# The first query products move into the feed-forward block, and statistics and splits change places, in a transformer kernel

## The reference, cut to what matters

```python
x = x + 0.5 * _L0_ffn_ref(_layernorm(x), ...)    # gated, 256 -> 768 -> 256
x = x + _L0_attn_ref(_layernorm(x), ...)         # 16 heads of 16
x = x + 0.5 * _L0_ffn_ref(_layernorm(x), ...)
x = x + 0.5 * _L1_ffn_ref(_layernorm(x), ...)    # gelu, 256 -> 1024 -> 256
x = x + _L1_attn_ref(_layernorm(x), ...)         # rotary, causal mask
x = x + 0.5 * _L1_ffn_ref(_layernorm(x), ...)
```

## Time and profile before

| what | value |
|---|---|
| median of 3 runs | 2131.1 us (2126.84 to 2133.12) |
| profiled execution, its own time | 2130.66 us |
| its span, first to last instruction | 2128.9 us |
| PE busy | 2003.7 us (94%) |
| DVE busy | 1652.5 us (78%) |
| ACT, POOL busy | 1317.6 us (62%), 510.8 us (24%) |
| mean granted TensorE clock | 0.976 of full speed |

### The profile page before, as it was taken

The page is one execution under the profiler, slowest core; times in us unless marked ns, Lnnn a source line. Parts: engine busy times, 40 slices in busy tenths (PEclk is TensorE's granted clock), DMA queues, the critical chain, the costliest instruction groups (busy, mean ns, idle before and its releaser), DMA issues. The chain is left out here.

```text
span 2128.9 us, 43472 instructions
## 1 busy us (share of the span) xinstructions
PE 2003.7 (94%) x16326; PEld 1246.8 (59%) x16326; DVE 1652.5 (78%) x2997; ACT 1317.6 (62%) x2560; POOL 510.8 (24%) x572
## 2 busy tenths in 40 slices
PE   4998989999999999998998999978999999989999
PEld 3887833333333333336887899864444444448998
DVE  7776699999999999937776545789999999927333
ACT  3443338888888888881444445544777777753544
POOL 2000141221241241142101211584321212122110
PEclk9999969999999999999999999997999999999999
DMA  4002844225335444313002000385465555310000
GB/s 149 1 0 81 313 87 74 47 52 100 77 67 91 73 85 79 49 51 111 1 0 65 1 0 1 114 277 117 91 113 103 118 108 104 87 54 27 20 20 30
DMA packets 124374, 161.63 MB, mean 76 GB/s; under 512 B 54668, under 2 KB 77900, under 8 KB 124180
## 3 DMA queue, kind: packets, MB, share of 16 engines
q1 hardware_dynamic: 101156, 112.32, 24.7%
q0 software_dynamic: 16256, 37.82, 6.7%
q10 hardware_dynamic: 6768, 8.91, 1.3%
HBM read 94.02 MB, written 63.70 MB: 74 GB/s over the span
## 5 line engine op out<-in xcount | busy, mean ns | idle before, releaser
L1630 ACT ACTIVATE att_probs<-att_s_exp 128x512 f32<-128x512 f32 (+3 forms) x1792 | 883.3, 551 | 201.1 <-PE att_s_exp L1528 160.0
L1665 DVE TENSOR_REDUCE maxes<-att_s_max 128x2 f32<-128x1024 f32 x640 | 771.6, 1223 | 32.6 <-PE att_s_max L1486 28.2
L1553 PE MATMUL att_o_ps<-att_probs,att_v_st 128*32 128x256 f32 (+2 forms) x6400 | 514.1, 393 | 10.2 <-ACT att_o_sb L1607 9.1
L1553 PEld LDWEIGHTS att_o_ps<-att_probs,att_v_st 128*32 128x32 f32 x6400 | 127.1, 108 | 253.1 <-issue 137.3
L1659 DVE CUSTOM_DVE_ANT_0 att_s_max<-att_s_max,mask_q 128x384 f32<-128x384 f32 (+3 forms) x512 | 235.6, 523 | 23.9 <-PE att_s_max L1486 21.6
L1528 PE MATMUL att_s_exp<-first_q,first_k 64*128 64x512 f32 (+3 forms) x672 | 177.8, 471 | 1.4 <-DMA first_q<-att_m_parts 0.8
L1486 PE MATMUL att_s_max<-first_k,first_q 62*128 62x512 f32 (+3 forms) x672 | 146.7, 435 | 22.9 <-DVE maxes L1665 11.6
L1528 PE MATMUL att_s_exp<-w_lo,w_hi 64*128 64x512 f32 x640 | 164.5, 497 | 1.2 <-DMA w_lo<-att_m_parts 1.2
L1749 POOL TENSOR_TENSOR att_m_parts<-m_turned,att_zeros 32x128 fp32r<-32x128 f32 x64 | 29.0, 453 | 496.7 <-ACT m_turned L1596 358.4
L1528 PEld LDWEIGHTS att_s_exp<-w_lo,w_hi 64*128 64x128 f32 x640 | 63.1, 183 | 133.9 <-ACT att_probs L1630 123.5
L1528 PEld LDWEIGHTS att_s_exp<-first_q,first_k 64*128 64x128 f32 x672 | 78.7, 189 | 100.5 <-ACT att_probs L1630 87.8
(11 more groups left out here) (322 smaller groups left out, 4368.2 us busy)
## 6 DMA issues: line engine op xcount, KB each, us to landing
attention_rows<-att_o_sb POOLq DMA_DIRECT2D x64, 256.0 KB, 4.5
output_wide<-attention_weights POOLq DMA_DIRECT2D x36, 256.0 KB, 5.6
first_q<-q_parts SPq DMA_DIRECT2D x132, 64.0 KB, 4.9
first_k<-k_parts SPq DMA_DIRECT2D x66, 128.0 KB, 4.5
q_parts<-qkv_parts SPq DMA_DIRECT2D x16, 512.0 KB
k_parts<-qkv_parts SPq DMA_DIRECT2D x16, 512.0 KB
att_v_raw<-v_rows SPq DMA_DIRECT2D x32, 256.0 KB, 5.7
output_o_t<-attention_rows POOLq DMA_DIRECT2D x16, 512.0 KB, 7.1
```

Source lines behind the costliest of these rows:

```text
L1553: mm = pe.matmul(o_ps[j * VW:(j + 1) * VW, cols], v_st[:, it.par, kt, j, :], probs[:, step % 2, j, cols], start=kt == 0 and opens, stop=st ...
L1630: act.activation(probs[:, step % 2, j, q0:512], s_exp[:, plan.bank[place], q0:512], ACT.Exp, scale=1.0 if causal else 0.25).then_inc(s["ex ...
L1665: v.tensor_reduce(maxes[:, qc, :, pairs, qt - 4 * qc, kc], banks, AX.X, ALU.max).then_inc(s["max_done"], 1)
```

## The change

Six things are changed at once. (1) `load_stage`: x chunk 1 is issued ahead of the gate weights. (2) POOL waits there for `xn_ready`, the first normalised chunk, before its splits. (3) In the following feed-forwards the norm steps are made for the tiles of six chunks (`FOLLOW`, 0 to 23), both in chunk 6: variance at slice 3, ahead of `part_lo`, reciprocal root at slice 5. (4) In `ffn0a` and `ffn1a` chunk 1 of the next stage is normalised before the last `finish`. (5) The accumulators `qk_ps` of the next stage are allocated around both blocks, the feed-forward's `up_ps` is a view of them, and PE makes the first two query tiles (`HEAD`) at the end of the feed-forward's block, after the test on `whole` is left. (6) `qkv_stage` and `rope_stage` start with the third tile; the norm of the last two chunks (`LATER`, 24 to 31) is split: variance in chunk 0 and root in chunk 2 of `qkv_stage`, variance in chunk 2 and root in chunk 3 of `rope_stage`.

```diff
-    body(CHUNKS - 3, 1, (CHUNKS - 3) // 2, False, False, "variance")
-    body(CHUNKS - 2, 0, (CHUNKS - 2) // 2, False, False, "rstd")
+    body(CHUNKS - 3, 1, (CHUNKS - 3) // 2, False, False)
+    body(CHUNKS - 2, 0, (CHUNKS - 2) // 2, False, False, True)
...
+FOLLOW = slice(0, 6 * CT)
+HEAD = KD
+LATER = slice(6 * CT, TILES)
...
+def qk_tile(pe, E, par, i):
+
+    w, half = (E.wq, E.wk)[i // KD], i % KD
+    for k in range(KD):
+        mm = three_pass(pe, E.qk_ps[:, i, :], pair(w, slice(None), k, slice(half * P, (half + 1) * P)),
+                        pair(E.xt, slice(None), par, k, slice(None)), k == 0, k == KD - 1)
+    return mm
...
             load_x(0)
+            load_x(1)
             split.load(sp, 0)
-            load_x(1)
...
             clear_operands(p, E)
+            p.wait_ge(s["xn_ready"], 1)
             for i in range(1, len(jobs)):
...
+        head = follow and xt_next is None
+        if head:
+            up_ps = E.qk_ps[:, 0:up_shape[1] * up_shape[2], :].rearrange("p (a g) n -> p a g n", a=2)
...
+            if head:
+                pe.wait_ge(used, CHUNKS * F)
+                pe.wait_ge(s["hi_ready"], CHUNKS * KD + KD)
+                pe.wait_ge(s["lo_ready"], CHUNKS * KD + KD)
+                pe.wait_ge(s["late_lo"], 2)
+                for i in range(HEAD):
+                    mm = qk_tile(pe, E, 0, i)
+                    if i % E.qk_step == E.qk_step - 1:
+                        mm.then_inc(E.qk_ready, 1)
...
-                    if f == 4 and follow and part == "variance":
-                        norm_variance(v, E, s["next_step"], NEXT)
-                    if f == 4 and follow and part == "rstd":
-                        norm_rstd(v, E, s["next_step"], NEXT, NORM_STEPS)
+                    if f == 3 and follow and next_norm:
+                        v.wait_ge(s["next_step"], 1)
+                        norm_variance(v, E, s["next_step"], FOLLOW, 1)
+                    if f == 5 and follow and next_norm:
+                        norm_rstd(v, E, s["next_step"], FOLLOW, 1 + NORM_STEPS)
...
+            if head:
+                v.wait_ge(s["turned"], CHUNKS * KD)
+                normalise(v, E, CHUNKS + 1, 1, s, rows=1)
             finish(CHUNKS - 1, (CHUNKS - 1) % 2)
...
 # qkv_stage
-                for i in range(QK):
+                for i in range(HEAD if first else 0, QK):
...
                 if opening(c):
-                    n = rest_variance(v, E, s)
-                    norm_rstd(v, E, s["ln_step"], REST, n)
+                    rest_variance(v, E, s, LATER)
+                elif isinstance(c, int) and c == 2:
+                    norm_rstd(v, E, s["ln_step"], LATER, 1 + NORM_STEPS)
...
 # rope_stage
-                for kind, w in enumerate((E.wq, E.wk)):
+                for kind in range(0 if c else HEAD // KD, KINDS):
...
-            count_front(v, E, s)
-            normalise(v, E, 1, 1, s)
-            n = rest_variance(v, E, s)
-            norm_rstd(v, E, s["ln_step"], REST, n)
-            v.tensor_scalar(neg_mean[:, :], E.mean[:, :], -1.0, None, ALU.mult).then_inc(s["means"], 1)
+            count_front(v, E, s, 2)
+            v.tensor_scalar(neg_mean[:, FOLLOW], E.mean[:, FOLLOW], -1.0, None, ALU.mult).then_inc(s["means"], 1)
...
+                if c == 2:
+                    n = rest_variance(v, E, s, LATER)
                 multiply(c, 1)
+                if c == 3:
+                    norm_rstd(v, E, s["ln_step"], LATER, n)
+                    v.tensor_scalar(neg_mean[:, LATER], E.mean[:, LATER], -1.0, None, ALU.mult).then_inc(s["means"], 1)
```

More of the change, by code:

```diff
@@ L492, in path @@
                     down(CHUNKS - 1, f, False)
-            if not gated:
-                path(False)
[L496 to L501, removed]
+            if gated:
+                whole = pe.value_load(E.whole[0:1, 0:1])
+                with pe.If(whole > 0):
+                    path(True)
+                with pe.Else():
+                    path(False)
+            else:
+                path(False)
+            if head:
[7 more added lines that the diff above has]
+                        mm.then_inc(E.qk_ready, 1)
         @block.scalar
@@ L594, in measure, with body @@
                     v.wait_ge(s["x_new"], c * 2 + 2)
-                    statistics(v, E, c)
-            def body(c, par, use, first, last, part=None):
+                    return statistics(v, E, c)
+            def body(c, par, use, first, last, next_norm=False):
                 if follow or not last:
@@ L625, in body @@
                     if f == BEHIND and not first:
-                        measure(c - 1)
+                        ins = measure(c - 1)
+                        if follow and next_norm:
+                            ins.then_inc(s["next_step"], 1)
                     if f < len(unmeasured) and first:
@@ L788, in start @@
             def start(c, par, use, last):
[L789 to L791 removed]
+                if not (last or opening(c)):
+                    v.wait_ge(s["turned"], c * KD)
                     normalise(v, E, c + 1, 1 - par, s)
@@ L910, in _ @@
                     for half in range(KD):
-                        for k in range(KD):
-                            mm = three_pass(pe, qk_ps[:, kind * KD + half, :], pair(w, slice(None), k, slice(half * P, (half + 1) * P)),
-                                            pair(E.xt, slice(None), par, k, slice(None)), k == 0, k == KD - 1)
+                        mm = qk_tile(pe, E, par, kind * KD + half)
                     mm.then_inc(s["qk_ready"], 1)
@@ L1963, in program @@
                        io["x"], io["ident"])
-            ffn_stage(nc, E, "ffn0a", True, late=square, follow=True)
-            late.close()
-            qkv_stage(nc, E, "qkv0")
+            with nc.psum_tensor("qk0", [P, 2 * KD, CHUNK], F32) as E.qk_ps:
+                E.qk_ready, E.qk_step = new_semaphore(nc, E, "qk0_ready"), 1
+                ffn_stage(nc, E, "ffn0a", True, late=square, follow=True)
+                late.close()
+                qkv_stage(nc, E, "qkv0")
             front.close()
@@ L2012, in program @@
                             (E.swap16[:, :], io["swap16"])], {0: 1.0 / HD})
-            ffn_stage(nc, E, "ffn1a", False, late=square, follow=True, issue=True, xt_first=xt_next)
-            late.close()
-            rope_stage(nc, E, "qkv1")
+            with nc.psum_tensor("qk1", [P, 2 * KD, CHUNK], F32) as E.qk_ps:
+                E.qk_ready, E.qk_step = new_semaphore(nc, E, "qk1_ready"), KD
+                ffn_stage(nc, E, "ffn1a", False, late=square, follow=True, issue=True, xt_first=xt_next)
+                late.close()
+                rope_stage(nc, E, "qkv1")
             front.close()
```

35 lines of the change are left out of this document (16 added, 19 removed).

## The result

| | median | runs | profiled execution (span) |
|---|---|---|---|
| before | 2130.9 us | 12, 2126.8 to 2133.3 | 2130.7 (2128.9) |
| after | 2126.3 us | 12, 2124.2 to 2129.0 | 2126.4 (2124.6) |

The ratio is 0.998, with a 95% interval of 0.9971 to 0.9989: 4.6 us faster, 0.2%. The forecast was 2120.0, 10.8 us faster. 2126.3 is inside the range on record (2111 to 2128), but the size was wrong by more than half, and by the bound of 0.3% it is "same", which had a chance of 0.14.

The account below looks back on a forecast made before the run. PE bounds the stages (in `qkv1` also POOL), so gains come only where it stands idle; -8.1 + 3.3 - 3.0 - 3.0 = -10.8 us from 2130.7 gives 2119.9, stated as 2120, range 2111 to 2128.

Parts of the forecast that it names:

- Part 1: Loading: earlier x chunk 1 and POOL's wait start DVE's work sooner, reductions keeping their lengths; -8.1 us.
- The rival in which the splits stay in DVE's way: Loading: reductions stretched beside POOL, loading gives 1 to 3 us, whole 4 to 6: 2126; chance 0.10.
- Part 2: Norm moved in chunk 6: +1.6 us in each gated feed-forward, +3.3 us charged for two; hidden in `ffn1a`.
- The stall for `h`: Chunk 7 of gated feed-forwards: PE waits 1.0 us for the first `h`, needed by `up` of slice 2.
- `finish`'s second half moves: Chunk 7 of `ffn0a`: from 170.67 to 172.3; PE already waits 0.6 us for it, so is later by 1.6 us.
- Part 3: First layer's join and `qkv0`: branch gap stays, chunk 1's wait shrinks, clock recovers, root steps hidden; -3.0 us.
- the clock in chunk 1: `qkv0`, 197.2 to 207: without the 2.1 us gap the 0.83 clock goes; -1.5 us counted.
- Part 4: Second layer's join and `qkv1`: block entered 1.2 us later, DVE's first multiply 5.3 us earlier, POOL bounds; -3.0 us.
- in chunk 2, statistics and 7 steps (2.9 us) come between: `qkv1` chunk 2, between `part_lo` and the second `multiply`: products at 1373.3, POOL still starting 3.4 us ahead.
- the root in chunk 3 takes another 2.6 us: `qkv1` chunk 3: 2.6 us of DVE before a pair that has over 3 us to spare.
- The moved norm costs more: Rival: clock falls in new gaps of chunk 7 and in `qkv1`'s chunk 2; 4 us more, 2124; chance 0.12.
- PE did not stay at half clock: Rival denied here: a `qkv1` stall leaves PE at half clock; 35 us would give 2137; chance 0.04.

Follow-up runs that it names:

- POOL held: Kernel after, but POOL waits while the norm steps run in chunks 2 and 3 of `qkv1`: 2119.3 us, ratio to before 0.9946.
- head in the arms: POOL held, plus the first layer's query products ahead issued at the end of both arms of the branch in `path`: 2120.2 us, ratio to before 0.9950.
- no head in layer 0: POOL held, but the first layer makes no query products ahead, all being made in `qkv0`: 2120.0 us, ratio to before 0.9954.
- old norm places: POOL held, but gated feed-forwards take norm steps where the kernel before did, the rest at the start of `qkv0`: 2119.7 us, ratio to before 0.9941.
- held in chunk 2 alone: Kernel after, but POOL waits for the norm steps only in chunk 2 of `qkv1`: 2125.6 us, ratio to before 0.9966.
- both of these: POOL held, plus the edits of head in the arms and old norm places together: 2122.0 us, ratio to before 0.9957.
- load only: Kernel before with the two loading edits alone (x chunk 1 ahead of gate weights, POOL's splits behind the first norm): 2121.0 us, ratio 0.9956.
- layer 0 as before: Kernel before with the loading edits and the second layer's part, POOL waiting at both stretches; first layer as before: 2117.5 us, ratio 0.9933.

## Why the prediction was right or wrong

**Part 1** was right: 8.24 us for 8.1, the reductions unstretched beside POOL, the start of `ffn0a` at 24.3 for 24.4. The rival in which the splits stay in DVE's way is out; that its 2126 is the time measured is chance, since the loss came from another stage.

**Part 2** had the right mechanism and a size somewhat too large: 1.27 and 0.92 us for 1.6 each. The stall for `h` is the 1.0 us forecast; the step "`finish`'s second half moves" cost PE less than its 0.6, since the wait for x stayed at 0.6 us in `ffn0a` and fell in `ffn0b`. The clock did not fall in chunk 7. What was called hidden in `ffn1a` is not where its 1.19 us went: they go with the longer stretch at half clock at its entry. In the seven traces with 6.8 us of it `ffn1a` is 0.9 to 1.6 us longer than before, in the five with 3.4 us between 0.2 shorter and 0.3 longer, among them kernels with the same code there (POOL held: -0.23; head in the arms: +0.02).

**Part 3** was right in each term: the gap 2.6 us and 0.3 more behind the head tiles (+0.3), 2.1 us to 0.2 (-1.9 for -1.8); with -2.76 in all, for -3.0, that leaves 1.2 for the clock in chunk 1, put at 1.5. That last term is the weak one: with the loading's edits alone the wait of 2.1 us stayed and no half clock followed it, so the gap does not bring it on each time, and part of the term may be luck. The gain does not need the head tiles: without them the stage ends within 0.1 us of the same time.

**Part 4** failed. Its first half held: the block is entered 1.15 us later against the end of `ffn1a` (1.2), and POOL's first instruction comes 5.55 us earlier (5.3). The step that failed is "in chunk 2, statistics and 7 steps (2.9 us) come between" and "the root in chunk 3 takes another 2.6 us": they measured 5.0 and 5.8 us. The steps' price was taken from the earlier trace rows, where POOL was busy for 5.7 of 151.5 us and where it had not begun; the steps were moved to where POOL is busy 68.6 of 75 us. The excess of the first, 2.1 us, is just what PE waits more than with POOL held (4.3 against 2.2), and the second's, 5.8 - 2.3, emptied the reserve of "over 3 us" on which the last step rested. Behind both waits came the half clock: for the clock the prediction had "up to 1.5 us more", and the stage ran 10.2 us at 1.2 GHz, some 4.5 us by the estimate above. With POOL out of the way the stage gave 3.2 us for the 3.0 forecast; with both stretches as they were it lost 3.2. The near agreement of 3.2 with 3.0 is in part luck: the six kernels that hold POOL at both places gave 1.7 to 3.3 us, 1.7 where a stretch at 1.2 GHz followed the wait of 2.2 us.

The Trainium skill (SBUF — State Buffer, Who interferes with whom) states this case: an instruction of VectorE with two inputs in SBUF contends with one of GpSimd that reads SBUF, and the ports that they share are an exclusive lock. The trace agrees: the step at L196 took 2.30 us instead of 0.17, up to the end of POOL's instruction. The prediction weighed that section for the loading's reductions alone, where it speaks for the change, and not for the steps, where it speaks against it.

**Rivals.** "The moved norm costs more" (2124) named `qkv1`'s chunk 2 and the clock, and came nearest; it did not have the wait for POOL. PE did not stay at half clock: it was back at 1.00 by 1396. What the runs leave open is the drift of unedited stages, below.

## What to carry to other kernels

The length of a small VectorE instruction depends on its place: before a chain of steps is moved, look at which engine runs beside the new place, and price a step that starts beside a GpSimd instruction at the rest of that instruction (2.30 us here), not at its own 0.17 us. If the chain must stand there, holding GpSimd for it costs the chain's length once (1.4 and 2.1 us here) instead of a wait that ends with GpSimd's instruction and empties GpSimd behind it. And take the sum of a many-part change apart: here two lines gave more than the whole, by the medians.

## What the runs showed of the hardware that was not expected

- Small instructions waited beside POOL even where they read one tensor alone: L218 (`tensor_scalar`, 1.22 us), L220 (which reads it twice, 2.31). Multiplies that read an accumulator (1.21), the statistics (1.40) and reductions did not.
- The same wait of PE was followed by a stretch at 1.2 GHz in one kernel and not in another. In chunk 2 of `qkv1`, behind 2.2 us: none in four kernels, 3.4 us of it in three (no head in layer 0, old norm places, held in chunk 2 alone). In `qkv0`, behind 2.1 or 2.2 us: in the kernel before, "old norm places" and "both of these", not in "load only" and "layer 0 as before". Behind 3.2 to 4.3 us in `qkv1` it came each time. So the length of a wait of 2 us does not tell by itself.
- The attention stage of the first layer with its output stage, the same code in every kernel, was between 1.7 us shorter and 2.6 us longer than before, and what follows the last matmul of `qkv1` between 0.7 shorter and 3.3 longer (the latter with POOL held in chunk 2 alone). Behind `qkv1`, counted from POOL's last instruction, the drift goes with the time that PE spent at 1.2 GHz: 37.9 us before; 36.8 to 37.5 in the seven kernels that are 0.4 to 1.2 us shorter there; 42.2 to 43.0 in the four that are 0.8 to 1.4 longer; 47.6 in the one that is 2.8 longer. A gain of 1 us in a stage can't be read from the end of this kernel. What makes PE spend more or less time at 1.2 GHz there was not tried.
- The gap at the branch out of `path` was 2.4 to 3.4 us in every kernel, wherever the products and norm steps stood.
